# A flamingo block on one core: silu, up halves and the last normalised rows moved in the hand-written order

## What is computed

```
xn  = layernorm(x)
q, k, v = xn Wq' + bq,  ctx Wk' + bk,  ctx Wv' + bv     # 32 query heads of 8, 8 groups of keys and values
w   = softmax(q k' / sqrt(8), causal and padding masks)
x   = x + tanh(g_x) * ((w v) Wo' + bo)
y   = layernorm(x)
s   = softmax(y Rw);  the two best of 16 experts, weights renormalised -> combine[token, expert]
x   = x + tanh(g_f) * sum_e combine[:, e] * ((silu(y Gate_e) * (y Up_e)) Down_e)    # 96 columns per expert
```

## Time and profile before

| | us |
|---|---|
| median of 3 runs | 245.51 (244.65 to 246.1) |
| the profiled execution | 244.14 |
| its span, first to last instruction | 242.3 |
| PE busy | 221.4 (91%) |
| DVE busy | 170.9 (71%) |
| ACT busy | 97.5 (40%) |
| POOL busy | 96.0 (40%) |

### The profile page before, as it was taken

The page is one execution under the profiler, slowest core; times in us unless marked ns, Lnnn a source line. Parts: engine busy times, 40 slices in busy tenths (PEclk is TensorE's granted clock), DMA queues, the critical chain, the costliest instruction groups (busy, mean ns, idle before and its releaser), DMA issues.

```text
span 242.3 us, 3821 instructions
## 1 busy us (share of the span) xinstructions
PE 221.4 (91%) x1279; PEld 159.5 (66%) x1279; DVE 170.9 (71%) x354; ACT 97.5 (40%) x191; POOL 96.0 (40%) x129
## 2 busy tenths in 40 slices
PE   0798798999999999999897979999999999999993
PEld 0675563465555554556354868888888798888892
DVE  2578978658777878776731767749976888784665
ACT  2366358756676766756675320021010101101000
POOL 6239325400709393935301030405996563420000
PEclk9999999999999999999999999999999999999998
DMA  6372320008751302021103100041547322112105
GB/s 192 94 233 57 77 54 22 4 0 189 165 140 29 68 0 50 18 65 28 39 8 130 46 0 0 0 136 51 144 108 197 113 89 68 62 46 87 43 0 173
DMA packets 26274, 18.33 MB, mean 76 GB/s; under 512 B 15600, under 2 KB 22320, under 8 KB 26256
## 3 DMA queue, kind: packets, MB, share of 16 engines
q1 hardware_dynamic: 25952, 17.87, 26.8%
q10 hardware_dynamic: 304, 0.22, 0.5%
HBM read 14.15 MB, written 1.11 MB: 63 GB/s over the span
## 4 chain that ended last, share of the span: by engine, by line
PE 69%; DVE 10%; POOL 6%; DMA 5%; ACT 3%; SPq 3%; issue 2%; ACTq 0%; DVEq 0%; POOLq 0%
PE bank L1010 64%; DVE mneg L874 3%; DMA wkv_n<-in_L_xattn_Wv 3%; SPq L429 2%; DMA w_t<-comb_d 1%; POOL cT L548 1%; PE bank L1070 1%; POOL w_d L552 1%; POOL cT L547 1%; POOL w_d L551 1%; DVE x_sb L1003 1%; DVE q L946 1%; DMA q<-q 1%; PE bank L1050 1%; PE bank L1083 1%
## 5 line engine op out<-in xcount | busy, mean ns | idle before, releaser
L1010 PE MATMUL bank<-xT,cT 128*128 128x512 f32 x288 | 70.1, 392 | 1.6 <-ACT pT L680 1.3
L1010 PEld LDWEIGHTS bank<-xT,cT 128*128 128x128 f32 x288 | 52.7, 188 | 12.4 <-issue 1.5
L874 DVE TENSOR_REDUCE mneg<-bank 128x4 f32<-128x512 f32 x64 | 43.0, 684 | 11.6 <-PE bank L1010 10.6
L693 ACT ACTIVATE pT<-bank 128x512 f32<-128x512 f32 x64 | 37.9, 599 | 19.2 <-PE bank L1010 18.2
L680 ACT ACTIVATE pT<-bank 128x512 f32<-128x512 f32 x24 | 14.4, 599 | 75.8 <-PE bank L1010 75.8
L1010 PE MATMUL bank<-w_d,q 128*128 128x256 f32 x288 | 38.5, 284 | 0.4 <-DVE q L948 0.4
L1010 PEld LDWEIGHTS bank<-w_d,q 128*128 128x128 f32 x288 | 36.9, 190 | 2.6 <-issue 1.2
L1010 PE MATMUL bank<-q,kz 112*128 112x512 f32 x64 | 37.3, 585 | 0.0
L934 DVE TENSOR_TENSOR pT<-pT,bank 128x512 f32<-128x512 f32 x24 | 16.4, 684 | 20.5 <-PE bank L1010 14.8
L1010 PE MATMUL bank<-kz,q 96*128 96x512 f32 x64 | 26.5, 419 | 2.4 <-DVE mneg L874 1.8
L478 POOL TENSOR_TENSOR vare<-mv,cst 128x1 f32<-128x1 f32 (+1 forms) x10 | 2.3, 233 | 59.5 <-DVE mv L728 52.7
(11 more groups left out here) (126 smaller groups left out, 278.7 us busy)
## 6 DMA issues: line engine op xcount, KB each, us to landing
w_t<-comb_d SPq DMA_DIRECT2D x16, 192.0 KB, 2.8
w_t<-comb_d SPq DMA_DIRECT2D x16, 128.0 KB, 2.9
padf<-in_L_ffn_down_w SPq DMA_DIRECT2D x12, 128.0 KB, 2.2
c_sb<-in_ctx SPq DMA_DIRECT2D x2, 512.0 KB, 6.7
q<-cT SPq DMA_DIRECT2D x8, 128.0 KB, 2.4
w_t<-comb_d SPq DMA_DIRECT2D x16, 64.0 KB, 2.7
out<-x_sb SPq DMA_DIRECT2D x4, 256.0 KB, 2.4
c_sb<-in_L_ffn_gate_w SPq DMA_DIRECT2D x8, 96.0 KB, 2.1
```

The costliest lines, as they stand in the source:

```text
L693: nc.scalar.activation(pT[:, i // 4, i % 4, :], bank[2 + s % 2][:], ACT.Exp, scale=SCALE).then_inc(p_done, 1)
L874: nc.vector.tensor_reduce(mneg[:, r, 4 * hf:4 * hf + 4], bank[SQ_BANK[n % 3]][:].rearrange("p (g k) -> p g k", g=4), X, ALU.max, negate=Tr ...
L1010: return nc.tensor.matmul(dst, a, b, start=start, stop=stop, skip_group_check=True)
```

## The change

Four things move; nothing but two small steps of POOL is added to or taken from what is computed, and one normalise changes its engine.

- best_two of half 0 is in slot 53 instead of 52, behind the copy of AT5.
- ACT does silu(0) in slot 64, ahead of the copy of the last values' product (slot 65). The gate half of unit 1 is in slot 64, ahead of TO7, its up half in 66; silu(1) in 66.
- Batch 7's rows are normalised by DVE at the start of slot 71, from mean and rstd, with a semaphore of their own; POOL leaves out nmr for them. YT7 is in slot 73, behind down(1), instead of 72, ahead of it.
- The gate half of unit 3 is in slot 73, behind YT7; SC1 in 74 instead of 73, ahead of the up half of unit 3. The silus get slots of their own in SILU_SLOT.

```diff
--- before.py
+++ after.py
@@ -215,6 +215,7 @@
         var_ok = sem("var_ok")
         rstd_ok = sem("rstd_ok")
         xn_ok = sem("xn_ok")
+        xn_last = sem("xn_last")
         brow_ok = sem("brow_ok")
 
         d_qn = [sem(f"d_qn{r}") for r in range(R)]
@@ -266,14 +267,14 @@
             if b:
                 AT_SLOT["MT", b] = G * b - 3
 
-            at = {0: (10, 13, 15, 18, 19), NB - 1: (9, 11, 13, 15, 16)}.get(b, (10, 12, 14, 18, 19))
+            at = {0: (10, 13, 15, 18, 19), NB - 1: (9, 11, 13, 15, 17)}.get(b, (10, 12, 14, 18, 19))
             for j, k in zip((("TO", b), ("AT", b), ("WO", b), None, ("YT", b)), at):
                 if j:
                     AT_SLOT[j] = G * b + k
                 else:
                     NORM_SLOT[b] = G * b + k
 
-        ROUTE = {"SC": (48, 73), "SN": (49, 75), "best": (52, 76), "weights": (55, 77), "CT": (58, 79)}
+        ROUTE = {"SC": (48, 74), "SN": (49, 75), "best": (53, 76), "weights": (55, 77), "CT": (58, 79)}
         for k in ("SC", "SN", "CT"):
             for h in range(NQ):
                 AT_SLOT[k, h] = ROUTE[k][h]
@@ -282,8 +283,10 @@
 
         LASTN = {t: max(n for n, (u, _) in enumerate(ORDER) if u == t) for t in range(FT)}
 
-        GATE_SLOT = 57
+
+        GATE_SLOT = {0: 57, 1: 64, 2: 70, 3: 73, 4: 77, 5: 80, 6: 81}
         UP_SLOT = {0: 64, 1: 66, 2: 70, 3: 74, 4: 77, 5: 80, 6: 81}
+        SILU_SLOT = {0: 64, 1: 66, 2: 71, 3: 75, 4: 78, 5: 81, 6: 82}
         WEIGH_SLOT = {0: 66, 1: 70, 2: 74, 3: 77, 4: 83}
         DOWN_SLOT = {0: 68, 1: 72, 2: 76, 3: 78}
         SLOTS = 84
@@ -477,7 +480,7 @@
                 pool.wait_ge(var_ok, k + 1)
                 step(pool.tensor_tensor(vare[:, t0:t0 + n], mv[:, t0:t0 + n, 1], cst[:, C_EPS:C_EPS + n], ALU.add))
                 power = pool.tensor_tensor(rstd[:, t0:t0 + n], vare[:, t0:t0 + n], cst[:, C_MH:C_MH + n], ALU.pow)
-                if k:
+                if 0 < k < NQ + NB - 1:
                     step(power)
                     step(pool.tensor_tensor(nmr[:, t0:t0 + n], mv[:, t0:t0 + n, 0], rstd[:, t0:t0 + n], ALU.mult))
                     pool.tensor_scalar(nmr[:, t0:t0 + n], nmr[:, t0:t0 + n], -1.0, None, ALU.mult).then_inc(rstd_ok, 1)
@@ -692,18 +695,20 @@
                         sc.wait_ge(pv_done, 2 * (b - 1) + i // 4 + 1)
                     nc.scalar.activation(pT[:, i // 4, i % 4, :], bank[2 + s % 2][:], ACT.Exp,
                                          scale=SCALE).then_inc(p_done, 1)
+                if s == SILU_SLOT[0]:
+                    silu(0)
                 if s % G == 1 and G < s < CH + G:
                     copy_o(s // G - 1)
                 if s in (4, 5):
                     for t in (2 * s - 4, 2 * s - 3):
                         normalise(1, t)
-                for b in range(NB):
+                for b in range(NB - 1):
                     if s == NORM_SLOT[b]:
                         if b == 0:
                             sc.wait_ge(d_qc[0], 16 * 3 * 4)
                         normalise(NQ + b, b)
-                for n, at in UP_SLOT.items():
-                    if s == at + 1:
+                for n, at in SILU_SLOT.items():
+                    if n and s == at:
                         silu(n)
             for n in range(len(UP_SLOT), len(ORDER)):
                 silu(n)
@@ -967,6 +972,10 @@
                     for t in range(TPH, NB):
                         ins = nc.vector.bn_aggr(mv[:, t], stats[:, t])
                     ins.then_inc(var_ok, 1)
+                if s == NORM_SLOT[NB - 1]:
+                    ve.wait_ge(rstd_ok, NQ + NB)
+                    nc.vector.tensor_scalar(xn[:, NB - 1], x_sb[:, NB - 1], mv[:, NB - 1, 0:1], rstd[:, NB - 1:NB],
+                                            ALU.subtract, ALU.mult).then_inc(xn_last, 1)
                 if s == 20:
                     ve.wait_ge(pool_init, 4)
                     ve.wait_ge(d_rw, 16)
@@ -1078,7 +1087,10 @@
                     ins = three(ps[:, 0:D], [lambda c, i=i: aT[i][:, c] for i in range(2)],
                                 [lambda c, i=i: wo[i][:, c] for i in range(2)], DC)
                 elif k == "YT":
-                    pe.wait_ge(xn_ok, 1 + TPH + j[1] + 1)
+                    if j[1] == NB - 1:
+                        pe.wait_ge(xn_last, 1)
+                    else:
+                        pe.wait_ge(xn_ok, 1 + TPH + j[1] + 1)
                     for c in range(DC):
                         ins = nc.tensor.transpose(ps[:, c * L:(c + 1) * L], xn[:, j[1], c * P:(c + 1) * P], ident)
                 elif k == "SC":
@@ -1198,13 +1210,11 @@
                     up(0, (1,))
                 if s % G == 0 and 0 < s <= CH:
                     weigh_values(s // G - 1, 1)
-                if s == GATE_SLOT:
-                    up(0, (0,))
                 for j in jobs_at(s):
                     job(j)
-                for n, at in UP_SLOT.items():
-                    if n and s == at:
-                        up(n)
+                for n in UP_SLOT:
+                    if s == GATE_SLOT[n] or n and s == UP_SLOT[n]:
+                        up(n, (0, 1) if GATE_SLOT[n] == UP_SLOT[n] else (0,) if s == GATE_SLOT[n] else (1,))
                 for n, at in DOWN_SLOT.items():
                     if s == at:
                         down(n)
```

## The result

The changed kernel takes 242.32 us, median of 6 (242.15 to 242.59), beside 244.80 for the kernel before (243.92 to 246.1, 6 runs). The ratio is 0.9897 (95%: 0.9870 to 0.9924), so it is 1.0% faster; 243.3 was forecast for the time and 2.25 us for the gain, against 2.5 measured between the medians. The profiled execution took 242.28, its span 240.5.

A forecast was written before the change was run, and what follows sets the result against it. The kernel was taken as PE work in order, gaining only where PE stands still ahead of the last full stretch. 0.40 + 1.85 = 2.25 us off the 245.51 median gave 243.3 us, range 242.1 to 245.0.

The forecast's parts named there:

- Part 1: best_two of half 0 from slot 52 to 53: WO5 loses its 0.65 us wait, gain 0.40 (bounds 0 and 0.65).
- Part 2: First silu ahead of the o_sb copy, unit 1 in halves: down(0) starts at 136.13 instead of 136.95, gain 0.82 us.
- Rival (a): Table load starts only when the copy did, silu(0) up to 1.77 us late, one for one: 245.0 us; chance 0.14.
- Part 3: Batch 7's rows on DVE, YT7 behind down(1): down(1) at 141.60 instead of 143.63, gain 2.03 us.
- Part 4: Gate half 3 covers YT7's copies ahead of SC1: down(3) at 152.25 instead of 154.10, so 1.85 of 2.03 us stay.
- The sum's last step: Behind down(3), POOL's splitting, SP's loads and DVE's waits move along; PE's 0.30 us wait stays, so 2.25 reaches the end.
- rival (c): Weight supply behind 166 us: three of four DVE waits grow by 1.5, PE loses 4.5: 247.8 us; chance 0.07.
- Margins (b): Part 1 gives nothing, margins of 0.1 at WO7 and 0.2 at SC1 each missed by 0.2: 244.05 us; chance 0.11.

The follow-up runs named there:

- the last kernel above: Changed kernel with gate half of unit 1 in slot 65, weigh(1) in 69, and SP issuing weight repeats ahead of tile loads: 240.26 us, ratio 0.9814 to the kernel before.
- the silu held back: Changed kernel with an unused 2048-column copy on ACT ahead of the first silu: 7 runs at 243.9 to 244.4 us, 5 at 245.1 to 245.8.
- the repeats first: Changed kernel with SP issuing the weight repeats of unit n ahead of the loads of tile n, tiles 8 to 11: 241.77 us.
- the two moves: Changed kernel with the gate half of unit 1 in slot 65, behind TO7, and weigh(1) in slot 69, ahead of the copy of WO7: 240.82 us.

## Why the prediction was right, point by point

**Part 1** was sized at 0.40. The product of slot 56 comes 0.43 earlier, and undoing the edit costs 0.39 at the median. The exps of slots 54 and 55 follow each other without a gap in the changed trace, as the step said.

**Part 2** was sized at 0.82 at down(0). Counted from the product of slot 64, down(0) was to start at 6.14 and does at 6.19, before at 6.96: 0.77. Experiment: 0.72 for the whole edit. The forecast "PE 1.1 before down(0), for DVE" holds as well. The bracket says 0.90 because it begins at the end of AT7's last matmul; by starts, down(0) is 1.28 behind AT7 (134.31 to 135.59), where it is 0.13 without a wait (135.09 to 135.22 in the last kernel above), so PE stands about 1.15.

**Rival (a)** fell with the first trace: the load starts directly behind the exp and lasts 1.28. Of the drain of about 1.38 that the Trainium skill (ScalarE: Activation LUTs, What ACT_TABLE_LOAD costs) adds, neither this trace nor the one with the silu held back shows anything ahead of the load or behind it: the gap before the load is 0.02 and 0.01. But the price that (a) put on a late silu, one for one, is what the held-back silu measured (1.77 for 1.89).

**Part 3**: down(1) was to start at 11.61 from the product and does at 11.71, before at 13.64. The step named both edits as one gain, and that is how it was; what it did not say, and the experiments show, is that each does most of it alone. Beside YT7's new place DVE's part could have been left out: the step gave it a price that was covered, and its gain is nothing.

**Part 4**: 1.85 was forecast to remain at down(3), 1.68 do. Of the missing 0.17, 0.10 was missing at down(1) already (11.71 for 11.61). The rest is the size of a half: I took 1.39 and 1.40, from SC1 in the kernel before, but gate half 3 takes 1.48 (142.76 to 144.24) and up half 3 1.46, while SC1 itself takes 1.38; YT7 gave 0.05 back. What the step did not say is that its gate half gains nothing over the kernel before, and only pays for part 3.

**The sum's last step was too simple.** "All of this hangs on CT1 or down(4), so it moves along and the 0.30 stays" was not borne out in the profiled execution, where PE's wait grew to 0.69. In the kernels with best_two back, with ACT's normalise, with YT7 ahead and with the gate half back it is 0.41, 0.30, 0.30 and 0.30, at about the same place, and in these four down(3) to the end is 88.2 to 88.4 us, as forecast. So it varies from one execution to another by some tenths, and isn't tied to the change. This is rival (c)'s mechanism, at a tenth of its price; SP's order is its cause, since it goes with the repeats first.

**What the sum didn't have** is the clock. It read 1.00 in the one profiled execution and I concluded "nothing can be bought back there". The profile is one execution and came from the lower group; the run list had 245.51 and 246.1 in it, which I took for scatter (under rival (c), even as a hint of supply trouble). Had I taken the difference from the profiled 244.14, the forecast would have been 241.9; from the median, 243.3, which is 1.0 too high, because two of those three runs were of the upper group. From the lower group's 244.5, known only afterwards, 2.25 leads to within 0.1 of the result, 242.32. That the forecast gain of 2.25 also lies near the 2.5 between the medians is in part luck: 2.2 of these are the order, and the rest comes from a clock that the sum held to be out of play. Margins (b) did not fail. Where the clock falls within such a run is in no trace here, since no profile was taken of one. That it has to do with the standstills around 130 to 135 us is shown by the edits that bring the group back and, less surely, by the one that takes it away; that it falls at that very place is only likely.

## What to carry to other kernels

Where one engine's work is a written-out order, sum the bracketed waits and ask for each what the late engine had in its queue ahead of the thing waited for; moving YT7 behind down(1) took a wait away, and moving a small step to another engine beside that gained nothing. When a job leaves its place, ask what had covered its copies there: here a half unit of PE's own work had to cover 1.25 us of them. Test each edit of a group alone, because two that remove the same wait count once, and one that only pays for another looks like a gain. And look at the spread of the runs before trusting one profile: here a third of them formed a group at a lower granted clock that the profile did not show.

## What the runs showed of the hardware

In this block short standstills of PE go with a lower mean clock, in a part of the executions only. Four kernels have long ones right behind the last values' product: the kernel before, best_two alone and the silu behind the copy with 0.80 and 1.28 within 2 us of each other, the held-back silu with 2.08. In them the mean granted clock is 0.993 or below in 40 of the 104 runs whose clock is known. In the other kernels PE stands there for 0.34 or 0.81 at most, or the gaps are filled, and a later wait of up to 1.42 (YT7) makes no difference: 5 of 77 runs, and the costliest of the five lies 1.1 us above its kernel's median. The 0.81 alone, with the two moves and with all three, left 1 of 12 runs at 0.993; the 1.28 alone was not tried. A run of an upper group takes about 1.4 us longer. I had expected one clock for every execution, as the profile shows 1.00 throughout the middle stretch.
